# Another merge of two phases' stages at the beginning, the three phase changes and the end of a four-layer graph network

## What is computed

```python
h = relu(layernorm(x)); x = x + L0(h, adj, ...)        # phase 0
h = relu(layernorm(x)); x = x + L1(h, adj, adj, ...)   # phase 1
h = relu(layernorm(x)); x = x + L2(h, adj, ...)        # phase 2
h = relu(layernorm(x)); x = x + L3(h, adj, ...)        # phase 3
# L0, for l in 0, 1:
#   u = (h Wl h') on and above the diagonal, (h Wr h') below it, / sqrt(384)
#   a = exp(u) * adj / (rowsum + 1e-10); h = relu(layer_norm(a @ (h Wlin + b)))
# L1, L2:
#   p = softmax(q k' * scale + bias) for each of 12 heads; out = (p v) Wo + bo
# L3, for l in 0, 1:
#   a = softmax(h h' / sqrt(384)) * adj, each row divided by its sum
#   c = (a above) hWl + diag(a) hWs + (a below) hWr; h = relu(layer_norm(c))
```

## Time and profile before

| | us |
|---|---|
| three runs | 2801.08, 2790.49, 2787.36 |
| median | 2790.49 |
| the profiled execution's span | 2789.9 |
| PE busy | 2736.0 (98%) |
| DVE busy | 2039.2 (73%) |
| POOL busy | 1455.7 (52%) |
| ACT busy | 1286.7 (46%) |

### The profile page before, as it was taken

How to read it: one execution, slowest core, us unless ns; L and a number is a source line. 1 busy time by engine, 2 the same in 40 slices (tenths; PEclk the granted TensorE clock), 3 DMA queues, 4 the chain that set the end, 5 groups by cost and what they waited for, 6 DMA issues and landing times.

```text
span 2789.9 us, 85742 instructions
## 1 busy us (share of the span) xinstructions
PE 2736.0 (98%) x34344; PEld 2535.4 (91%) x34344; DVE 2039.2 (73%) x4000; ACT 1286.7 (46%) x2069; POOL 1455.7 (52%) x2499
## 2 busy tenths in 40 slices
PE   9999999999999999999989999998999999999998
PEld 8999999999988999999889999998888888888887
DVE  5666666666687777777777777778667777777776
ACT  4343343433444444445444444444545545445453
POOL 2212221122225555555554555555677877778777
PEclk9999999999999999999999999999999999999999
DMA  3221111212112111111131111111112112111121
GB/s 122 77 83 41 63 61 41 83 41 67 58 55 85 49 49 49 52 52 49 39 107 46 52 49 49 49 49 64 39 39 75 38 41 72 38 62 51 38 75 35
DMA packets 116556, 159.19 MB, mean 57 GB/s; under 512 B 8048, under 2 KB 112368, under 8 KB 116464
## 3 DMA queue, kind: packets, MB, share of 16 engines
q1 hardware_dynamic: 116464, 157.88, 17.3%
HBM read 107.52 MB, written 50.33 MB: 57 GB/s over the span
## 4 chain that ended last, share of the span: by engine, by line
PE 90%; DVE 4%; POOL 2%; issue 2%; ACT 1%; DMA 1%; SPq 0%; POOLq 0%; DVEq 0%; ACTq 0%
PE ps L337 68%; PE ps L1863 3%; PE ps L1337 3%; PE ps L1319 3%; PE ps L935 3%; PE ps L1352 3%; PE ps L958 2%; PE ps L1841 2%; PE ps L871 2%; PE ps L1247 1%; PE ps L1780 1%; POOL wide L1511 1%; PE ps L1849 0%; DVE w_lo L409 0%; DVE wide L1198 0%
## 5 line engine op out<-in xcount | busy, mean ns | idle before, releaser
L337 PE MATMUL ps<-w_hi,split 128*128 128x384 f32 x4608 | 1267.1, 344 | 9.8 <-ACT wide L1113 5.3
L337 PEld LDWEIGHTS ps<-w_hi,split 128*128 128x128 f32 x4608 | 841.0, 189 | 28.7 <-ACT wide L1113 5.7
L337 PE MATMUL ps<-split,w_hi 128*128 128x256 f32 x4608 | 858.6, 282 | 0.6 <-ACT wide L682 0.6
L337 PE MATMUL ps<-w_lo,split 128*128 128x384 f32 x2304 | 780.2, 339 | 0.0
L337 PEld LDWEIGHTS ps<-split,w_hi 128*128 128x128 f32 x4608 | 719.7, 188 | 20.4 <-issue 19.6
L337 PE MATMUL ps<-split,w_lo 128*128 128x256 f32 x2304 | 583.2, 282 | 0.0
L337 PEld LDWEIGHTS ps<-w_lo,split 128*128 128x128 f32 x2304 | 434.9, 189 | 2.5 <-issue 2.1
L337 PEld LDWEIGHTS ps<-split,w_lo 128*128 128x128 f32 x2304 | 433.6, 188 | 1.3 <-issue 1.2
L1084 POOL TENSOR_TENSOR wide<-wide 128x192 f32<-128x192 f32 x256 | 214.0, 865 | 372.1 <-ACT wide L1147 372.1
L1511 POOL TENSOR_TENSOR wide<-wide,row 128x192 f32<-128x192 f32 x512 | 328.9, 676 | 22.2 <-ACT wide L1594 21.6
L651 POOL TENSOR_TENSOR rstd<-mv,pos_half 128x2 f32<-128x2 f32 x64 | 45.9, 725 | 439.4 <-DVE mv L835 439.4
(11 more groups left out here) (141 smaller groups left out, 4534.8 us busy)
## 6 DMA issues: line engine op xcount, KB each, us to landing
x_after<-wide SPq DMA_DIRECT2D x96, 384.0 KB, 2.5
xin<-x_after SPq DMA_DIRECT2D x96, 384.0 KB, 3.4
xin<-in_x SPq DMA_DIRECT2D x32, 384.0 KB, 4.1
wide<-in_x SPq DMA_DIRECT2D x32, 384.0 KB, 3.6
wide<-x_after SPq DMA_DIRECT2D x32, 384.0 KB, 4.1
out<-wide SPq DMA_DIRECT2D x32, 384.0 KB, 2.8
...
```

Source lines behind the costliest of these rows:

```text
L337: mm = nc.tensor.matmul(out, t if tokens_stay else w, w if tokens_stay else t, start=(k == 0), stop=(k == len(pairs) - 1))
```

## The change

Every string of BEGINNING, of BETWEEN[0] to [2] and of ENDING has the same stages as before in another order (products are also cut into thirds at other places, so that the count of words differs by a few). The three loops' strings, all functions and SyncE's order are the same. All twenty strings differ; from two of them, the start of DVE's in BEGINNING and of DVE's in BETWEEN[2]:

```diff
-    "stat.0 w0 split_0.0 w1 stat.1 w2 soft_0.0 att_0.0 split_0.1 lin_0.0 sum_0.0 agg_0.0 w3 ln_0.0 "
...
+    "stat.0 stat.1 split_0.0 w0 w1 w2 soft_0.0 att_0.0 split_0.1 lin_0.0 sum_0.0 agg_0.0 ln_0.0 w3 w4 "
...
-        "stat.0' abs.0'' fac.0'' v.1'' w0 w1 hT.0' pv.0'' s.1'' soft.1'' stat.1' abs.1'' fac.1'' "
-        "hT.1' pv.1'' v.0' s.0' soft.0' abs.0' stat.0 fac.0' v.1' s.1' soft.1' pv.0' abs.1' fac.1' "
...
+        "stat.0' abs.0'' fac.0'' w0 v.1'' hT.0' pv.0'' s.1'' soft.1'' stat.1' abs.1'' fac.1'' v.0' hT.1' "
+        "pv.1'' s.0' w1 soft.0' abs.0' fac.0' v.1' stat.0 s.1' soft.1' pv.0' abs.1' fac.1' stat.1 split_0.0 "
```

More of the change, by code:

```diff
@@ L63 @@
 ATT_ORDERS = [
-    "q0.1' q1.1' q2.1' k0.1' k1.1' v0.1' v1.1' pt0.0' hT.0 pt1.0' k2a.1' pt2.0' k2bc.1' pv.0' "
-    "scores.1' out0.0' out1.0' q0.0 q1.0 q2.0 k0.0 k1.0 v0.0 v1.0 pt0.1' hT.1 pt1.1' k2a.0 pt2.1' "
-    "k2bc.0 pv.1' scores.0 out0.1' out1.1'",
-    "q.1' norm.0 pt0.0' hT.0 pt1.0' pt2.0' k.1' pv.0' out.0' exp.1' q.0 norm.1 pt0.1' hT.1 pt1.1' "
-    "pt2.1' k.0 pv.1' out.1' exp.0",
-    "stat.0 abs.0' fac.0' v.1' hT.0 pv.0' s.1' soft.1' stat.1 abs.1' fac.1' v.0 hT.1 pv.1' s.0 "
-    "soft.0",
+    "q0.1' q1.1' q2.1' k0.1' k1.1' v0.1' v1.1' pt0.0' hT.0 pt1.0' k2a.1' pt2.0' k2bc.1' pv.0' scores.1' "
+    "out0.0' out1.0' q0.0 q1.0 q2.0 k0.0 k1.0 v0.0 v1.0 pt0.1' hT.1 pt1.1' k2a.0 pt2.1' k2bc.0 pv.1' "
+    "scores.0 out0.1' out1.1'",
+    "q.1' norm.0 pt0.0' hT.0 pt1.0' pt2.0' k.1' pv.0' out.0' exp.1' q.0 norm.1 pt0.1' hT.1 pt1.1' pt2.1' k.0 "
+    "pv.1' out.1' exp.0",
+    "stat.0 abs.0' fac.0' v.1' hT.0 pv.0' s.1' soft.1' stat.1 abs.1' fac.1' v.0 hT.1 pv.1' s.0 soft.0",
     "bias.1' stat.0 bias.0 p.0' xb.1' out.0' stat.1 p.1' xb.0 out.1'",
```

## The result

The changed kernel takes 2803.45 us (median of 7 runs, 2798.28 to 2807.03), the kernel before 2790.8 us (7 runs, 2787.36 to 2801.08). The ratio is 1.0036 with the interval [1.002, 1.0052]: slower by 0.36%, some 10 us by the ratio and 12.7 by the medians. That is within the 0.5% that I had called "same", which had 0.95, but above the range of 2786 to 2799 us, and clear of zero where I had forecast +1.4 us. The prediction was wrong.

The account below looks back on a forecast made before the run. TensorE was taken to bound the kernel, busy 2736.0 of 2789.9 us. Terms 4.2 + 1.7 - 2.5 - 1.3 - 1.0 + 0.3 = +1.4, plus 0.6 to the runs' median, gave 2791.9 us; range 2786 to 2799.

Parts of the forecast that it names:

- phase change 0 to 1: Between phases 0 and 1: waits for ACT's copies of k and others shrink, a later softmax chain costs 0.5; -2.5 us.
- 2 to 3: Last phase change: w1 leaves its place ahead of pv.0'', ending a 1.6 us wait; s.1' starts 0.5 us earlier; -1.0 us.
- The opening: Kernel start: DVE's stat.1 waits for x, w0 ends later, first product at 16.9 us; +4.2 us and +1.7 of clock.
- The waits' share: Opening: first product 5.0 us later, less 0.7 and 0.4 given back, plus 0.3 for a subtraction; +4.2 us.
- The clock's term: Opening: PE idles 5.6 us in one piece, so the granted clock drops once; +1.7 us, bounds 0 and 3.4.
- 1 to 2: Second phase change: the q.1 wait moves to pt0.0, s.0 starts earlier, a copy wait shrinks by 0.7; -1.3 us.
- rival 2: Last phase change: SP waits for w1, x lands late, s.1' and out0.0' wait, clock drops; 2797.0 us, chance 0.2.
- My own sign of being wrong: Last phase: stat.0 running after 1941 us would show the forecast wrong; it was expected at about 1939.
- The end: Behind the last layer's statistics: DVE waits 0.35 us for POOL, other moves nearly cancel; +0.3 us.
- Rival 1: Phase changes give 3.5, 2.5 and 3, the end 0.5, the opening costs 3 without clock; 2784.0 us, chance 0.15.
- Rival 3: Loops' first rounds: issue waits and their low clocks move or vanish, up to 6 us either way; chance 0.05.

Follow-up runs that it names:

- e13: The changed kernel with 52 instead of 8 unused matmuls behind the first transposes alone; 2812.22 us, ratio 1.0066 to the kernel before.
- e9: The changed kernel with POOL's stat.0 ahead of stat.1 again in the change from phase 0 to 1; one run, 2798.56 us against 2790.84 before.
- e3: The kernel before with only the changed order of the phase change 1 to 2; 2792.59 us, ratio 1.0003 to the kernel before.

## Why the prediction was wrong

Two terms of the sum failed in their mechanism: the phase change 0 to 1, by 7.7 us, and 2 to 3, by 6.2. The rest was right or is within what executions differ.

- **The opening** was right in its mechanism. First product at about 16.9: measured 17.06. hT_0.1 in u_0.0's wait: 0.90 became 0.2. Half of the 0.81 ahead of hT_1.0: 0.5 is left. The waits' share was 4.2; idle time grew by 3.6. The clock's term, 1.7 us, was too small for this execution, where the fall lasted 10.2 us and cost 2.7 to 2.9, and right for those where it lasted 6.8. The rule of the Trainium skill that I had cited for it ("TensorE: Matmul & The Clock Gate", Part 1: The HAM clock gate) is borne out by e13, where PE was kept busy and the clock stayed at 1.00. I had 5.9 for the opening; it is 6.7 in this trace and 5.9 in the mean of all. The opening is not what made the forecast wrong.
- **Phase change 0 to 1, -2.5 forecast, +5.2 measured.** The waits that I took away did go (L1118 2.7 to 0.9, L1220's 0.7). The step that failed is the sentence on POOL: "norm.0 comes some 3 us later, still about when hT.0 is wanted, which I count as nothing". It cost 2.6 us of waiting, and e9's trace has 4.7 of the 5.2 us back by this one swap, with one fall of the clock less (against the mean of all traces 3.9 of 4.0). I had priced POOL's stat from undisturbed instructions, and had not laid it beside DVE's three splits, for which the Trainium skill ("SBUF — State Buffer", Who interferes with whom) has the rule.
- **1 to 2, -1.3 forecast.** The trade was as said: the 2.8 us on q.1 vanished, 3.2 us appeared at pt0.0, and the 1.7 on pt2's copy became 0.8. Not in the sum were an issue wait of 1.4 us inside the uncut scores.0' and 10.2 us at half clock: +2.5 in this trace, and +0.3 in the mean of all. e3 by itself measured 1.0003 [0.9989, 1.0017], which leaves room for my -1.3. The -5.8 behind it, in the first round, is chance as far as the runs tell.
- **2 to 3, -1.0 forecast, +5.2 measured.** This is my rival 2, to which I gave 0.2: its place, its chain (w1, SP, xb.0', x, stat.0, s.1', pv.0' behind soft.1'), the clock's fall, and 5.1 us above the forecast, 6.2 in fact. It lacked ACT's queue, where norm.0 holds the copy of pv.0' as long. What failed in the forecast is the time of x, "asked for at about 1934.8". I had let xb.0' follow out.1'' on POOL at once. But it waits for the store of iteration 14, which SP issued right behind 1152 KB of weights, and which POOL waited for until 6.7 us after its issue. x was asked for 6 us later than I had it (the 8.8 us taken off), against a slack of about 1 us; 3.2 of the 6 are POOL's wait for the store; out.1'' began 2.3 us later than my time implied, and xb.0' took 2.76 us and not 2.25. The weights were asked for at 1930.5 by that count and not at 1927; with them at 1927 and 6.5 us for the store, it would have landed just ahead of the end of out.1'' (an estimate). My own sign of being wrong, stat.0 of the last phase after 1941, was there: 1953.33, or 1944.6 by that count.
- **The end, +0.3**: +0.28 to the last matmul, and +0.4 to the end of the span.
- **The sum's form.** I added one fall of the clock for the whole kernel. The change has 27 us more at 0.50, of which the opening has 10. The trace of before had shown it: falls behind waits of 1.3 to 2.6 us, and waits of 2.5 and 2.8 us without one. I took from this that such waits may be borne; it means that each has some chance of one, in these traces 77 of 139.
- Rival 1 (0.15) was wrong. Rival 3 (0.05) had a real mechanism: issue waits did move, by +2.2 us in the sum of the trace, and the first round of phase 2 became 5.8 us shorter, with the clock. But they move as much between other traces (6.0 to 11.0 us), so no difference between the two kernels can be laid to them.
